# Two summing steps of the attention heads on GpSimd, ternary weights turned by DMA, and theta projected in the loading stage

## What is computed

```python
x = x + tanh(g_xattn[0]) * L0_xattn(ctx, ctx, layernorm(x), ssm_kernel, D, 8)   # H3-like heads
x = x + tanh(g_ffn[0])   * L0_ffn(layernorm(x), w1, b1, w2, b2)                  # int8 quantised
x = x + tanh(g_xattn[1]) * L1_xattn(layernorm(x), ctx, theta, phi, g, ln, out)   # softmax attention
x = x + tanh(g_ffn[1])   * L1_ffn(x_normalised, w1, g1, w2, g2, w3, g3)          # ternary weights

# L0_xattn, per head h (32 heads of 8 rows) and batch element b:
kv[i, j, l]  = k[i, l] * v[j, l]                       # k = v = ctx, so kv is symmetric in i, j
y            = causal_conv(kv, ssm_kernel[h]) + kv * D[h]
out[j, l]    = sum_i y[i, j, l] * q[i, l]
# L1_xattn
theta_x = theta_w @ input2 + theta_b ;  phi_x = phi_w @ input1 + phi_b    # input2 = ctx
scores  = theta_x^T phi_x ; p = softmax(scores) ; t_x = p @ g_x ; layernorm, relu, out_w, + input2
# L1_ffn weights
wq = round(tanh(w / (mean|w| + eps))) * arctanh(mean|w|)
```

## Time and profile before

| | us |
|---|---|
| median of three runs | 809.2 |
| profiled execution | 809.86 |
| its span, first to last instruction | 808.0 |
| TensorE busy | 680.9 (84%) |
| VectorE busy | 680.9 (84%) |
| ScalarE busy | 500.9 (62%) |
| GpSimd busy | 316.7 (39%) |

### The profile page before, as it was taken

How to read it: one execution, slowest core, us unless ns; L and a number is a source line. 1 busy time by engine, 2 the same in 40 slices (tenths; PEclk the granted TensorE clock), 3 DMA queues, 4 the chain that set the end, 5 groups by cost and what they waited for, 6 DMA issues and landing times.

```text
span 808.0 us, 11857 instructions
## 1 busy us (share of the span) xinstructions
PE 680.9 (84%) x3476; PEld 402.4 (50%) x3476; DVE 680.9 (84%) x1172; ACT 500.9 (62%) x816; POOL 316.7 (39%) x372
## 2 busy tenths in 40 slices
PE   3659888598888919998879799999889999999996
PEld 3546665366656714453334555555534444444443
DVE  3776999859999666896979768888999999999993
ACT  3873654235443849799453654444548888888884
POOL 3534555245543420120941200101245655555552
PEclk9969999889999969999989999999999999999999
DMA  8953656347885320215585000000000000000000
GB/s 303 311 187 128 210 189 201 110 133 231 243 238 189 133 76 3 101 52 208 209 264 174 9 1 1 0 0 0 1 0 14 26 13 26 13 26 26 13 26 27
DMA packets 50046, 83.18 MB, mean 103 GB/s; under 512 B 6432, under 2 KB 19488, under 8 KB 48864
## 3 DMA queue, kind: packets, MB, share of 16 engines
q1 hardware_dynamic: 45664, 74.43, 27.6%
q10 hardware_dynamic: 4352, 8.39, 3.4%
HBM read 68.04 MB, written 14.76 MB: 102 GB/s over the span
## 4 chain that ended last, share of the span: by engine, by line
DVE 32%; PE 32%; issue 14%; ACT 14%; POOL 4%; DMA 3%; DVEq 1%; SPq 0%; POOLq 0%; ACTq 0%
DVE turn L1374 11%; PE ps L983 4%; PE ps L1060 4%; PE ps L1025 4%; ACT arena L907 3%; PE ps L1167 3%; PE ps L1134 3%; DVE arena L1664 3%; ACT turn L800 2%; DVE q L1669 2%; ACT arena L754 2%; PE ps L1114 2%; DVE arena L1752 2%; PE ps L1127 2%; PE ps L1119 2%
## 5 line engine op out<-in xcount | busy, mean ns | idle before, releaser
L983 PE MATMUL ps<-arena 128*128 128x288 f32 x640 | 168.2, 421 | 36.9 <-DVE turn L1363 26.4
L983 PEld LDWEIGHTS ps<-arena 128*128 128x128 f32 x640 | 122.9, 196 | 82.0 <-issue 32.0
L1205 PE MATMUL ps<-arena 128*128 128x512 bf16 x512 | 116.2, 380 | 9.2 <-ACT arena L883 7.6
L555 POOL TENSOR_TENSOR arena<-arena 128x512 f32<-128x512 f32 x64 | 87.9, 1376 | 68.8 <-DVE arena L1752 68.8
L461 POOL TENSOR_TENSOR arena<-arena 128x1024 f32<-128x1024 f32 x32 | 60.8, 1899 | 103.6 <-ACT arena L642 79.2
L1374 DVE TENSOR_TENSOR turn<-turn 128x1024 f32<-128x1024 f32 x64 | 98.3, 1536 | 0.0
L1205 PEld LDWEIGHTS ps<-arena 128*128 128x128 bf16 x512 | 47.5, 98 | 71.4 <-issue 14.3
L654 ACT ACTIVATE arena<-arena 128x512 f32<-128x512 f32 (+1 forms) x32 | 20.0, 629 | 97.2 <-DVE turn L1363 97.2
L1060 PE MATMUL ps<-arena 128*128 128x512 bf16 x256 | 59.6, 396 | 10.8 <-DVE arena L1541 8.1
L1223 PE MATMUL ps<-arena 128*128 128x512 bf16 x256 | 61.7, 386 | 0.0
L1349 DVE TENSOR_TENSOR turn<-ps,arena 128x1024 f32<-128x1024 f32 x32 | 39.2, 1225 | 26.4 <-PE ps L983 23.1
(11 more groups left out here) (205 smaller groups left out, 1410.5 us busy)
## 6 DMA issues: line engine op xcount, KB each, us to landing
arena<-in_L_ffn_w SPq DMA_DIRECT2D x72, 256.0 KB, 3.9
arena<-kpad_d ACTq DMA_DIRECT2D x16, 512.0 KB, 5.4
late<-in_L_ffn_w SPq DMA_DIRECT2D x24, 256.0 KB, 4.7
tern_d<-late SPq DMA_DIRECT2D x48, 128.0 KB, 3.6
arena<-in_x SPq DMA_DIRECT2D x4, 1024.0 KB, 12.6
arena<-in_ctx SPq DMA_DIRECT2D x4, 1024.0 KB, 13.6
arena<-in_L_ffn_w SPq DMA_DIRECT2D x4, 1024.0 KB, 11.1
x_d<-arena SPq DMA_DIRECT2D x4, 1024.0 KB, 4.1
```

The lines of the kernel that those rows point to most:

```text
L555: pool.tensor_tensor(hg[:, s, sl], hh[:, s, sl], g3[:, sl], ALU.mult).then_inc(S["hg_done"], 1)
L983: last = pe.matmul(ps[:, 4 * s + lo, 0:NB * PAIRS], toep[:, u, (lo - li) * P:(lo - li) * P + P], kv[:, s, li, :], start=(li == 0), stop=(l ...
L1205: last = pe.matmul(ps[:, 3 + 2 * j + c % 2, :], xq4T[:, s, 4 * j + k, :], w[:, k, c * L:(c + 1) * L], start=(k == 0), stop=(k == LB - 1))
```

## The change

In the heads, `near` becomes a product written back into PSUM, after `far` and `opposite` have written their products into a tile `pd` of half the former size. One VectorE addition, PSUM plus `pd`, writes `half[u]`. The last two halvings, 16 and 8, go to GpSimd (`add_halves`). VectorE works one head at a time. The ternary values are still rounded by the write to int16, but ScalarE then copies them to bf16 (`widen`), after the tanhs of the whole batch; only the copy raises `tern_used`, and SP stores the bf16 values. The twelve turns on TensorE with their widening and copying are taken out; SP issues twelve DMA transposes from DRAM, four before the second product of the first feed-forward network has ended, eight after it and ahead of the gains. TensorE waits for all of them ahead of the first `up`. Theta's weight and bias are loaded with the first inputs, the eight theta projections go between the input transposes, ScalarE copies them into a new tile `theta`, and in attention it copies from there. The other projection weights keep their place.

```diff
@@ near, far, opposite, halve, head_pair -> head
+            def head(h, u):
+                pd, qd = prod[u], qdup[:, u]
+                y = ps[:, 4 * u:4 * u + 4, 0:NB * PAIRS].rearrange("p l (b n) -> p l b n", n=PAIRS)
                 v.wait_ge(S["y_ready"], h + 3)
                 v.wait_ge(S["qd_ready"], h + 1)
+                dv.done(v.tensor_tensor(spread(pd[:, :, 1:], [[32, ROWS], [9, 3], [1, 8]]), y[:, :, :, 8:32],
+                                        spread(qd, [[16, ROWS], [0, 3], [1, 8]]), ALU.mult))
+                v.tensor_tensor(spread(pd, [[32, ROWS], [9, 4]]), y[:, :, :, 32:36],
+                                spread(qd[:, :, 4:], [[16, ROWS], [1, 4]]), ALU.mult)
+                v.tensor_tensor(pd[:, :, 28:32], y[:, :, :, 32:36], spread(qd, [[16, ROWS], [1, 4]]), ALU.mult)
+                dv.wait()
+                dv.done(v.tensor_tensor(y[:, :, :, 0:32], y[:, :, :, 0:32],
+                                        spread(qd, [[16, ROWS], [1, 4], [1, 8]]), ALU.mult))
+                dv.wait()
                 v.wait_ge(S["o_done"], h + 1)
+                v.tensor_tensor(half[u], y[:, :, :, 0:32], pd, ALU.add).then_inc(S["prod_done"], 1)
@@ GpSimd
+            def add_halves(h, u):
+                pool.wait_ge(S["prod_done"], h + 3)
+                x = half[u]
+                po.done(pool.tensor_tensor(x[:, :, 0:16], x[:, :, 0:16], x[:, :, 16:32], ALU.add))
+                po.wait()
+                pool.tensor_tensor(qT[:, :, ds(HD * h, HD)], x[:, :, 0:8], x[:, :, 8:16], ALU.add).then_inc(S["o_done"], 1)
+
+            pool.wait_ge(S["pj_ready"], NB)
             pairs(0, 0)
...
             pairs(1, 1)
-            with pool.Fori(1, HEADS // 4) as i:
+            pairs(2, 0)
+            with po.loop(6, 2) as i:
                 for u in range(2):
-                    pairs(2 * i + u, u)
+                    add_halves(2 * i + u, u)
+                    pairs(2 * i + u + 3, 1 - u)
             pool.wait_ge(S["bsum_ready"], 1)
             pool.partition_all_reduce(stot[:, :], scol[:, :], P, RED.add).then_inc(S["bsum_all"], 1)
...
@@ ScalarE, ternary values
-                act.activation(tint[:, n, :], traw[n], ACT.Tanh, scale=inv_s[:, w:w + 1]).then_inc(S["tern_used"], 1)
+                ac.done(act.activation(tint[:, n, :], traw[n], ACT.Tanh, scale=inv_s[:, w:w + 1]))
+            def widen(k):
+                ac.wait()
+                act.activation(tbf[:, k % 4, :], tint[:, k % 4, :], ACT.Copy).then_inc(S["tern_used"], 1)
...
+                    for k in range(first, last):
+                        ternary(k)
+                    for k in range(first, last):
+                        widen(k)
@@ ScalarE, start
+            def th_copy(b):
+                act.wait_ge(S["pj_ready"], b + 1)
+                act.activation(theta[:, b, :], ps[:, 1 + b % 3, :], ACT.Identity, bias=cols3[:, 0:1]).then_inc(S["th_out"], 1)
             for t in range(NT):
...
+                if t >= 5 and t % 2 == 1:
+                    th_copy((t - 5) // 2)
+            for b in (NB - 2, NB - 1):
+                th_copy(b)
...
+            act.wait_ge(S["pj_ready"], NB)
             repeat_c(0, 0)
@@ ScalarE, attention
             def proj_out(b, p):
-                act.wait_ge(S["pj_ready"], 3 * b + 1)
-                act.activation(thT[:, p, :], ps[:, 0, :], ACT.Identity, bias=cols3[:, 0:1])
-                act.wait_ge(S["pj_ready"], 3 * b + 2)
+                if not (isinstance(b, int) and b <= 1):
+                    act.wait_ge(S["sc_ready"], 4 * (b - 1))
+                act.activation(thT[:, p, :], theta[:, ds(b, 1), :].rearrange("p a t -> p (a t)"), ACT.Copy)
+                act.wait_ge(S["pj_ready"], NB + 2 * b + 1)
@@ TensorE, start
+            def project_ctx(b):
+                pe.wait_ge(S["w3_out"], 1)
+                pe.wait_ge(c_in[b // 2], 16)
+                if b >= 3:
+                    pe.wait_ge(S["th_out"], b - 2)
+                for d in range(2):
+                    last = pe.matmul(ps[:, 1 + b % 3, :], thw[:, 2 + d, :], ctx_nat[:, 2 * b + d, :], start=(d == 0), stop=(d == 1))
+                last.then_inc(S["pj_ready"], 1)
             for t in range(NT):
...
+                if t >= 4 and t % 2 == 0:
+                    project_ctx((t - 4) // 2)
+            for b in (NB - 2, NB - 1):
+                project_ctx(b)
             for c in range(4):
                 pe.wait_ge(S["wqb_ready"], c + 1)
+                if c == 0:
+                    pe.wait_ge(S["th_out"], NB)
@@ TensorE, before attention, in attention, before the second feed-forward network
-            for k in range(7):
-                tern_T(k)
...
             def project(b, p):
                 pe.wait_ge(S["x3_done"], 2 * b + 2)
-                for d in range(2):
-                    last = pe.matmul(ps[:, 0, :], wT3[:, d, :], ctx3[:, ds(2 * b + d, 1), :].rearrange("p a t -> p (a t)"),
-                                     start=(d == 0), stop=(d == 1))
-                last.then_inc(S["pj_ready"], 1)
...
             project(0, 0)
-            for k in range(7, 12):
-                tern_T(k)
...
+            pe.wait_ge(S["bw_in"], 16 * 12)
             pe.wait_ge(S["xT_out"], 1)
             up(0, 0, (0, 1))
@@ SP
+                    sp.dma_start(thw[:, 0:2, :], theta_w_d.rearrange("l (d k) -> l d k", d=2)).then_inc(S["w3_in"], 16)
+                    sp.dma_start(cols3[:, 0:1], theta_b_d.rearrange("(p o) -> p o", o=1)).then_inc(S["late_in"], 16)
...
                 if c >= 2:
                     sp.wait_ge(S["c_rev"], G * (c + 1))
+                    sp.wait_ge(S["pj_ready"], 2 * c + 2)
                 sp.dma_start(raw[c].rearrange("p (j k) -> p j k", j=4), w1c[c]).then_inc(w_in[c], 16)
...
             sp.dma_start(beta, beta_d).then_inc(S["late_in"], 16)
+            def turned(dst, w, n):
+                rows = tern_d[w].rearrange("(f k) -> f k", k=L if w < 2 else FF)
+                src = rows[n * L:(n + 1) * L, :] if w < 2 else rows[:, n * L:(n + 1) * L]
+                sp.dma_start_transpose(dst, src).then_inc(S["bw_in"], 16)
+            for n in range(4):
+                turned(bw1T[:, :, n * L:(n + 1) * L], 0, n)
             sp.wait_ge(S["mm2_done"], NT)
+            for n in range(4):
+                turned(bw2T[:, :, n * L:(n + 1) * L], 1, n)
+            for n in range(4):
+                turned(bw3T[:, 4 * n:4 * n + 4, :], 2, n)
             sp.dma_start(g3, bcast_rows(bg3_d, FF)).then_inc(S["gs_in"], 16)
```

201 lines of the change are left out of this document (50 added, 151 removed).

## The result

The changed kernel takes **814.2 us** (median of 20 runs, 811.6 to 821.2), the kernel before 809.9 us (20 runs, 806.2 to 812.9): ratio 1.0054, 95% interval 1.0038 to 1.0070. It is slower, by little. I had forecast 791.5 us, a range of 768 to 812 and 0.18 for slower; the median lies outside the range.

A forecast was written before the change was run, and what follows sets the result against it. No engine bounds all of it: VectorE is busy 98% in the head loop, TensorE 100% in attention. 809.9 + 7.6 (heads over) - 17.3 (ternary turn) - 8.1 (attention) = 792.1 us, against the median 791.5; range 768 to 812.

The forecast's parts named there:

- the end of the heads: After head 31, ending at 267.0 us against 259.4 before (+7.6), the turning back on TensorE follows without a gap.
- VectorE's and GpSimd's costs: Per head, VectorE takes 3.9 us in place of 6.1, GpSimd 4.25; both fit under TensorE's 4.95.
- rival 5: In the heads, VectorE and GpSimd still block each other: pitch 6.1 us, kernel 807 us; chance 0.03.
- Start, +13: Theta projections among the input transposes make the first head start at 69 us, 13 late; lower end 7, upper 17.
- First half at TensorE's pitch: Heads before the partition sum follow each other at TensorE's 4.95 us, after three at the cold rate, 17.75 us.
- Partition sum, 10 us idle: GpSimd's one partition sum, between the halves of the heads, stops it for 13 us and leaves TensorE idle 10 us.
- The second half's ring at 7.3 us per head: Ternary tiles' four slots: a tanh waits for an earlier tile's copy and store, 7.3 us per head where before 6.1.
- Rival 3: Second half of the heads: stores land in 5 us behind Toeplitz loads, 1.4 us x 14 more, 811 us; chance 0.12.
- Ternary turn, -17.3: Before attention, without TensorE's twelve turns of ternary weights, scores(0) starts at 447.5 us instead of 464.82: -17.3 us.
- Transposes at no cost: Twelve DMA transposes of 2 to 5 us each lie hidden beside attention; cover breaks above 9.2 us each.
- Attention, -8.1: Without theta's projection TensorE needs 14.06 us per batch element; VectorE takes over at 14.7; -8.1 us in all.
- the chance of 0.79 for faster: Whole kernel: chance of beating the kernel before, against 0.03 for the same and 0.18 for slower.

The follow-up runs named there:

- e1: The changed kernel with the gated identity made on GpSimd before the last two heads' sums, not after them: 803.4 us, ratio 0.9935.
- e9: The changed kernel with eight slots instead of four for loaded ternary tiles, four kept for stored ones: 810.2 us, ratio 1.0007.
- e10: The changed kernel with eight slots instead of four for stored ternary tiles, four kept for loaded ones: 806.2 us, ratio 0.9974.
- e3: The changed kernel with theta projected in the attention stage again, as in the kernel before: 804.9 us, ratio 0.9957.
- the last two: The f3 kernel, and the same with every second bf16 copy on VectorE and loads signalled by the tanh: 748.2 and 747.6 us.
- the last kernel: The f3 kernel with every second bf16 copy on VectorE, loads signalled by the tanh and stores by the copy: 747.6 us, ratio 0.9241.
- f3: The changed kernel with theta in attention, gated identity early, copies behind tanhs, Toeplitz room, partition sum by matmul, eight load and store slots: 748.2 us.

## Why the prediction was wrong

It missed by 23.4 us of span (-17.8 against +5.6). The step that failed is the end of the heads: after head 31 the turning back was to start at once, and it waited for an instruction in GpSimd's queue, 10.4 us of the 23.4 with what follows. With that one instruction moved (e1, the gated identity early) the kernel takes 803.4 us, inside the range. The rest is made up of smaller misses. By its own steps:

- **VectorE's and GpSimd's costs**: right. 1.23 for the in-place product (1.22 measured), 1.9 for GpSimd's two sums (1.28 and 0.72, with the wait 2.1), no mutual blocking (rival 5 out). Alone, the split is worth 12.7 us.
- **Start, +13**: 13.8, right in sum (pairs of tiles 4.8 us apart instead of 5.1).
- **First half at TensorE's pitch**: 2 us too short; the magnitudes' ring of four load slots was in none of my rows. e9 shows it.
- **Partition sum, 10 us idle**: 11.0.
- **The second half's ring at 7.3 us per head**: right in mechanism and nearly in size: nine batches at 7.64 on average, and 6.86 around the one shown. Rival 3 (811) names a time near the measured one by another cause, and is out: the stores landed in 3.8 us (median, 5.0 at most), near the 3.6 of the forecast. But I counted one ring, and there are two (e9, e10). Its total was 5 us short, 3.9 of them in the first interval: the first batch starts at 160.4 and the second only at 171.6, as its repeats wait for VectorE's head 15.
- **The end of the heads**: this step failed. I wrote that the last pairs and the last head follow the start of the last batch, which they do (268.10, pairs at 268.27), and then let the turning back start at once. I had followed GpSimd's queue for the pairs but not past them: the gated identity, untouched by the diff, now stands behind sums that wait for VectorE. 7.8 us of gap and 2.4 at the lower clock behind it (e1).
- **Ternary turn, -17.3**: -15.5. The projections ahead of scores(0) found TensorE idle and at a low clock (0.83 from 468 to 478): with theta late it is -16.8, at a clock of 1.00.
- **Transposes at no cost**: right. They landed in 5.0 us (median, 8.5 at most), at the upper end of my 2 to 5, and overlap: 3.3 us each over the twelve, against the 9.2 at which the cover would have broken. The Trainium skill's figure ("DMA: Bandwidth & Descriptors", effective bandwidth of DMA_TRANSPOSE), from which I had estimated 2.0 us each, is above what this trace shows: 6.3 MB in 40 us are 157 GB/s, with the DMA engines busy throughout. No run isolates why.
- **Attention, -8.1**: -9.9, near in size by a wrong mechanism. VectorE did not take over: TensorE stayed full, elements 14.45 us apart (scores at 504.45 and 518.90). But from the last scores to the end it takes 2 us longer (233.8 against 231.6), which I had at nothing. TensorE waits 2.98 us for ScalarE's exponentials there, where it had waited 1.48, and its next sixteen transposes take 3.40 us instead of 2.21. This belongs to theta early (e3).
- The first feed-forward took 2.1 us longer (137.9 against 135.8), at a granted clock of 0.96 instead of 0.99 in its first product. Its instructions are the same in all the kernels, and it took 135.1 to 138.0 us in them, 135.2 and 137.3 in the last two: this difference is no larger than what the stage shows by itself.

The sum of misses: 0.8 (start) + 7.9 (heads) + 8.0 (gap, counted from head 31's end) + 2.4 (clock behind it) + 2.1 + 1.8 (scores) - 1.8 (attention) + 2.2 (end) = 23.4. Of the heads' 7.9, the first half has 2.1, the partition sum 1.0 and the ring 4.8.

And a judgement apart from the terms: the chance of 0.79 for faster rested on two gains that were sure and on losses that I had each priced at their known part only. The end of the loop was in no rival at all.

## What to carry to other kernels

When work is moved to another engine's queue, read that queue on to its next consumer behind the loop: an instruction that nobody touched can become the last one that everybody waits for. When a signal moves behind an added step, list everything that hangs on it, here a load and a store, and count the slots of each; widening one of two nearly equal rings gave 4 and 8 us here, and both together 31. A wait that an engine shows may be a symptom of the engine that issues the transfer: first give the issuer its time back.

## What the runs showed of the hardware

A **cast on VectorE beside GpSimd** takes anything from 0.28 to 1.40 us. The rows of the last kernel for the copies of 128x512 from int16 to bf16 (least, median, most, in ns):

```profile
L1360 DVE CAST late<-late x12: 282/453/1399, 138.2 to 201.3; 128x512 bf16<-128x512 int16 x12
L1360 DVE CAST arena<-arena x12: 282/283/1396, 143.4 to 206.3; 128x512 bf16<-128x512 int16 x12
```

I had expected 0.25. The products and sums with one operand in PSUM, beside the same GpSimd work, keep 1.22 to 1.23 us. The Trainium skill, "SBUF — State Buffer" (Who interferes with whom), says that a cast can take the port pair which VectorE shares with GpSimd, and that an instruction with one SBUF input outside those modes does not; by that rule the spread is time spent waiting for a GpSimd instruction, and the trace agrees: the cast of 1.40 us starts at 148.06, right behind the start of a GpSimd sum (148.02, 1.28 us long), and ends 0.16 us after it, while one that starts at 143.36, ahead of the next such sum (143.52), takes 0.28.

**TensorE's granted clock** follows its gaps. It is 0.75 over the stretch that begins with 7.8 us of idle time, and the first two matmuls there take 2.08 us, twice the 1.02 without the gap. In the stretch where heads waited for their pairs some took 6.8 us and others 5.1. In f3, where no head waits for longer than 0.35 us, the clock is 1.00 from 60 to 214.

**DMA transposes** of 0.5 MB keep SP for 1.9 to 6.0 us each, twelve of them 33.8 us: other transfers on that queue would have had to wait.
